# New call orders for the five engines of an attention and feed-forward kernel

## The reference

```python
q, k, v = x @ wq, x @ wk, x @ wv
q, k = rope(q) * D**-0.5, rope(k) * D**-0.5     # half of the features are rotated
p = softmax(causal_mask(q @ k.T))               # one head of 128
x1 = layernorm(x + (p @ v) @ wo)
w1b = mean(abs(w1), axis=1) * sign(w1)          # binarized weights, w2 alike
h = gelu(x1 @ w1b.T + b1)
out = layernorm(x1 + h @ w2b.T + b2)
```

## Time and profile before

| | |
|---|---|
| median of 3 runs | 276.72 us (276.22 to 276.80) |
| profiled execution: span | 274.5 us |
| PE busy | 260.9 us, 95% of the span |
| PE weight loads | 208.7 us, 76% (beside the matmuls) |
| DVE busy | 229.6 us, 84% |
| ACT busy | 224.7 us, 82% |
| POOL busy | 167.2 us, 61% |
| DMA | 31.94 MB, mean 116 GB/s |
| chain that ended last | PE 81%, DVE 6%, ACT 5%, issue 3%, DMA 2% |

### The profile page before, as it was taken

The page is one execution under the profiler, slowest core; times in us unless marked ns, Lnnn a source line. Parts: engine busy times, 40 slices in busy tenths (PEclk is TensorE's granted clock), DMA queues, the critical chain, the costliest instruction groups (busy, mean ns, idle before and its releaser), DMA issues.

```text
span 274.5 us, 5184 instructions
## 1 busy us (share of the span) xinstructions
PE 260.9 (95%) x1485; PEld 208.7 (76%) x1487; DVE 229.6 (84%) x638; ACT 224.7 (82%) x398; POOL 167.2 (61%) x258
## 2 busy tenths in 40 slices
PE   7899999999999999999999999999999999999960
PEld 3678989987779588868879688868886878897630
DVE  2799999999999996999979987998689738537984
ACT  3378964565897989996998999898999799999972
POOL 3033132613625698399821998497819887887772
PEclk9999999999999999999999999999999999999997
DMA  7944596479657936833685318825830720200323
GB/s 178 166 61 87 107 145 98 115 163 192 104 132 160 199 94 153 180 47 78 173 187 127 82 39 249 184 71 151 189 73 27 197 55 2 76 2 0 111 90 108
DMA packets 58012, 31.94 MB, mean 116 GB/s; under 512 B 33408, under 2 KB 54400, under 8 KB 57984
## 3 DMA queue, kind: packets, MB, share of 16 engines
q1 hardware_dynamic: 57024, 30.76, 50.4%
q10 hardware_dynamic: 960, 0.85, 1.3%
HBM read 9.18 MB, written 4.19 MB: 49 GB/s over the span
## 4 chain that ended last, share of the span: by engine, by line
PE 81%; DVE 6%; ACT 5%; issue 3%; DMA 2%; ACTq 1%; POOL 0%; POOLq 0%
PE pair L589 18%; PE bank L606 18%; PE bank L632 5%; PE bank L674 4%; PE pair L650 4%; PE pair L651 4%; PE bank L620 4%; PE bank L682 4%; PE bank L683 4%; PE bank L719 2%; DMA sin_sb<-in_sin_dram 2%; PE pair L663 2%; PE pair L665 2%; PE pair L664 2%; PE bank L639 2%
## 5 line engine op out<-in xcount | busy, mean ns | idle before, releaser
L391 POOL TENSOR_TENSOR hid_lo<-hid,hid_hi 128x1024 fp32r<-128x1024 f32 x28 | 66.0, 2386 | 19.7 <-ACT hid_hi L1075 19.7
L1004 ACT ACTIVATE prob<-pair,negmax 128x128 f32<-128x128 f32 (+3 forms) x64 | 47.2, 742 | 14.2 <-DVE negmax L1457 12.5
L606 PE MATMUL bank<-probT,xa 128*128 128x512 f32 (+3 forms) x160 | 54.2, 482 | 0.0
L1457 DVE CUSTOM_DVE_ANT_0 pair<-pair,mask_row 128x128 f32<-128x128 f32 (+3 forms) x64 | 47.9, 759 | 6.1 <-PE pair L589 5.5
L606 PEld LDWEIGHTS bank<-probT,xa 128*128 128x128 f32 x160 | 29.1, 190 | 20.2 <-issue 15.3
L341 POOL TENSOR_TENSOR xT_lo<-xT,xT_hi 128x512 fp32r<-128x512 f32 x14 | 18.0, 1288 | 40.4 <-ACT xT_hi L1034 40.4
L1467 DVE STREAM_TRANSPOSE turned<-prob 128x128 f32<-128x128 f32 (+7 forms) x56 | 39.5, 724 | 0.5 <-ACT prob L1004 0.5
L589 PE MATMUL pair<-qkT_hi 128*128 128x512 f32 (+3 forms) x96 | 36.0, 375 | 0.8 <-DVE qkT_lo L1619 0.3
L1068 ACT ACTIVATE hid<-pair,b_sb,alpha 128x1024 f32<-128x1024 f32 x28 | 32.9, 1209 | 0.1
L589 PE MATMUL pair<-qkT_lo,qkT_hi 128*128 128x512 f32 (+3 forms) x96 | 32.8, 342 | 0.0
L589 PE MATMUL pair<-qkT_hi,qkT_lo 128*128 128x512 f32 (+3 forms) x96 | 32.8, 342 | 0.0
(11 more groups left out here) (116 smaller groups left out, 649.9 us busy)
## 6 DMA issues: line engine op xcount, KB each, us to landing
probT<-turned SPq DMA_DIRECT2D x96, 116.0 KB, 2.3
probT<-turned SPq DMA_DIRECT2D x128, 52.0 KB, 2.0
xq<-in_L_attn_x_dram SPq DMA_DIRECT2D x28, 128.0 KB, 4.0
xa<-in_L_attn_x_dram SPq DMA_DIRECT2D x7, 512.0 KB, 4.7
out_dram<-res SPq DMA_DIRECT2D x7, 512.0 KB, 3.3
hid<-in_L_ffn_w_dram SPq DMA_DIRECT2D x2, 256.0 KB, 3.2
out_dram<-res SPq DMA_DIRECT2D x2, 256.0 KB, 2.3
xa<-in_L_attn_x_dram SPq DMA_DIRECT2D x1, 256.0 KB, 3.6
```

Of the source, the lines that this page charges most:

```text
L391: pool.tensor_tensor(hid_lo[:, j, :], hid[:, j, :], hid_hi[:, j, :].bitcast(F32), ALU.subtract).then_inc(s_hid_lo[j], 1)
L606: ins = pe.matmul(bank_of["px", g, c][:, 0:n * P], xa[c % 2][:, j, :], probT[g][:, :, TG * j:TG * j + n, :].rearrange("p n m i -> p m n i" ...
L1004: act.activation(prob[r % 3][:, 0:(r + 1) * P], pair_of["score", r, c][:, slice(*columns(r))], ACT.Exp, scale=-1.0, bias=negmax[:, r:r + 1 ...
L1457: dve.tensor_tensor_reduce(mine, mine, mask_row[:, T - (r + 1) * P:T], -1.0, -MASKED, ALU.add, ALU.min, negmax[:, r:r + 1]).then_inc(s_max ...
```

## The change

Every engine's list has the same calls as before, in another order. The only other edit is a condition in `fill`, which is now also called before three pairs have been handed out. The full diff is some 900 lines long; below are all of SP, the opening of POOL, and those parts of the other lists of which the text speaks.

```diff
@@ -255,10 +255,10 @@
                 sp.dma_start(out[c].rearrange("(n p) d -> p n d", p=P)[:, ts, :], res2[c % 2][:, ts, :]
                              ).then_inc(s_stored[c % 2], 16)
 
+            tokens(1)
             stripes(2)
             carry(0, 0)
             stripes(3)
-            tokens(1)
             stripes(B - 4)
             carry(0, 1)
             carry(1, 1)
@@ -269,22 +269,22 @@
             stripes(B - 2)
             tokens(3)
             carry(0, 3)
+            stripes(B - 1)
             carry(1, 3)
-            stripes(B - 1)
+            tokens(B - 4)
             carry(0, B - 4)
-            tokens(B - 4)
-            tokens(B - 3)
+            store(0)
             carry(1, B - 4)
             carry(0, B - 3)
+            tokens(B - 3)
             tokens(B - 2)
-            store(0)
             carry(1, B - 3)
+            store(1)
             carry(0, B - 2)
-            store(1)
+            tokens(B - 1)
             carry(1, B - 2)
+            carry(0, B - 1)
             store(2)
-            tokens(B - 1)
-            carry(0, B - 1)
             store(3)
             store(B - 4)
             store(B - 3)
@@ -400,48 +400,48 @@
             rotation_sum(0, 2)
             xT_low(0, 3)
             xT_low(1, 3)
+            rotation_sum(1, 2)
             first_factors(0, 0)
-            rotation_sum(1, 2)
+            first_factors(1, 0)
             rotation_sum(0, 3)
-            first_factors(1, 0)
             xT_low(0, B - 4)
-            xT_low(1, B - 4)
             rotation_sum(1, 3)
             first_factors(0, 1)
+            xT_low(1, B - 4)
             first_factors(1, 1)
             rotation_sum(0, B - 4)
-            rotation_sum(1, B - 4)
             hidden_low(0, 0)
             hidden_low(1, 0)
+            xT_low(0, B - 3)
+            xT_low(1, B - 3)
             hidden_low(2, 0)
-            xT_low(0, B - 3)
             hidden_low(3, 0)
+            rotation_sum(1, B - 4)
+            hidden_low(0, 1)
             first_factors(0, 2)
-            xT_low(1, B - 3)
             first_factors(1, 2)
+            second_factors(0)
             rotation_sum(0, B - 3)
+            rotation_sum(1, B - 3)
...
@@ -556,7 +556,8 @@
 
             def fill(n):
 
-                wait_freed(*list(pair_of)[-len(pairs)])
+                if len(pair_of) >= len(pairs):
+                    wait_freed(*list(pair_of)[-len(pairs)])
                 for _ in range(n):
                     pe.matmul(pairs[len(pair_of) % len(pairs)][:, 0:BANK], warm[:, 0:P], warm[:, :], start=True, stop=True)
 
@@ -730,15 +731,15 @@
             turn_qk(1, 0)
             keep_warm(6)
             setup_turn_wv()
+            fill(2)
             scores(0, 0)
             scores(1, 0)
-            fill(2)
+            scores(2, 0)
+            setup_wvo()
             turn_qk(2, 0)
-            scores(2, 0)
             scores(3, 0)
-            setup_wvo()
+            turn_qk(3, 0)
             project(0, 1)
-            turn_qk(3, 0)
             project(1, 1)
...
             up(3, 0)
             scores(0, 3)
+            weigh_group(0, 0, 3, 2)
+            turn_x1(0, 1)
             scores(1, 3)
-            turn_qk(3, 3)
-            weigh_group(0, 0, 3, 2)
             scores(2, 3)
-            turn_x1(0, 1)
             scores(3, 3)
+            project_out(0, 2)
             scores(4, 3)
-            project_out(0, 2)
             project(1, B - 4)
             scores(5, 3)
+            turn_x1(1, 1)
+            weigh_group(1, 0, 3, 2)
+            weigh_group(1, 4, 7, 2)
             scores(6, 3)
-            weigh_group(1, 0, 3, 2)
-            turn_x1(1, 1)
-            weigh_group(1, 4, 7, 2)
             scores(7, 3)
             turn_qk(0, B - 4)
             turn_qk(1, B - 4)
             up(0, 1)
             up(1, 1)
             project_out(1, 2)
+            down(0, 0)
+            down(1, 0)
...
             weigh_row(6, B - 1)
+            turn_x1(0, B - 1)
             weigh_row(7, B - 1)
-            turn_x1(0, B - 1)
+            up_half(0, 0, B - 1)
             project_out(1, B - 1)
-            up_half(0, 0, B - 1)
             up_half(0, 1, B - 1)
             down(0, B - 2)
             down(1, B - 2)
             turn_x1(1, B - 1)
-            fill(7)
             turn_y(0, B - 2)
             turn_y(1, B - 2)
-            fill(2)
             up_half(1, 0, B - 1)
             up_half(1, 1, B - 1)
             down_quarter(0, 0, B - 1)
@@ -982,6 +981,8 @@
             down_quarter(2, 1, B - 1)
             down_quarter(3, 1, B - 1)
             turn_y(1, B - 1)
+            fill(7)
+            fill(2)
 
         @block.scalar
...
             xT_high(0, 1)
-            setup_signs()
+            xT_high(1, 1)
             exponentials(0, 0)
             exponentials(1, 0)
-            xT_high(1, 1)
             exponentials(2, 0)
-            exponentials(3, 0)
             qkT_high(2, 0)
             qkT_high(3, 0)
+            exponentials(3, 0)
+            setup_signs()
             setup_magnitudes()
...
             tok_copy(1, B - 3)
-            pxT_copy(0, 3)
+            second_norm(0, 0)
+            second_norm(1, 0)
+            second_norm(2, 0)
+            second_norm(3, 0)
+            x1T_high(0, 2)
             xT_high(0, B - 2)
-            xT_high(1, B - 2)
-            hidden_high(1, 1)
-            hidden_high(2, 1)
             exponentials(2, B - 4)
             exponentials(3, B - 4)
             exponentials(4, B - 4)
+            xT_high(1, B - 2)
+            x1T_high(1, 2)
+            hidden_high(2, 1)
             hidden_high(3, 1)
+            pxT_copy(1, 3)
             exponentials(5, B - 4)
-            pxT_copy(1, 3)
-            x1T_high(0, 2)
-            x1T_high(1, 2)
+            second_norm(4, 0)
+            second_norm(5, 0)
+            second_norm(6, 0)
             exponentials(6, B - 4)
+            second_norm(7, 0)
...
             gelu(2, 3)
-            gelu(3, 3)
-            tok_copy(0, B - 1)
-            y_half(1, 2)
-            exponentials(0, B - 2)
-            exponentials(1, B - 2)
-            hidden_high(0, 3)
-            pxT_copy(0, B - 3)
-            xT_high(1, B - 1)
-            exponentials(2, B - 2)
-            exponentials(3, B - 2)
-            exponentials(4, B - 2)
             second_norm(0, 1)
-            x1T_high(0, B - 4)
             second_norm(1, 1)
-            hidden_high(1, 3)
-            hidden_high(2, 3)
-            hidden_high(3, 3)
-            x1T_high(1, B - 4)
             second_norm(2, 1)
             second_norm(3, 1)
             second_norm(4, 1)
+            gelu(3, 3)
+            y_half(0, 2)
+            tok_copy(0, B - 1)
+            second_norm(5, 1)
+            y_half(1, 2)
+            second_norm(6, 1)
...
             second_norm(1, 2)
             second_norm(2, 2)
+            second_norm(3, 2)
+            second_norm(4, 2)
+            second_norm(5, 2)
             tok_copy(1, B - 1)
+            y_half(0, 3)
             y_half(1, 3)
-            second_norm(3, 2)
             gelu(2, B - 4)
+            second_norm(6, 2)
+            second_norm(7, 2)
...
@@ -1630,34 +1631,33 @@
             x_squares(0, 1)
             qkT_low(0, 0)
             qkT_low(1, 0)
-            first_rotation_sum(1)
+            x_squares(1, 1)
             setup_wvT()
             row_max(0, 0)
+            first_rotation_sum(1)
             row_max(1, 0)
-            x_squares(1, 1)
+            row_max(2, 0)
+            setup_wvo()
...
             rotate(0, 2)
-            row_max(2, 1)
             turn_row(0, 1)
             turn_row(1, 1)
+            row_max(2, 1)
+            row_max(3, 1)
             x_squares(0, 3)
             x_squares(1, 3)
-            row_max(3, 1)
             turn_row(2, 1)
             row_max(4, 1)
+            reciprocals(1, 0)
             turn_row(3, 1)
             row_max(5, 1)
-            turn_row(4, 1)
+            row_max(6, 1)
             residual1(0, 0)
             residual1(1, 0)
             residual1(2, 0)
             residual1(3, 0)
+            row_max(7, 1)
+            qkT_low(0, 2)
             statistics1(0, 0)
-            turn_row(5, 1)
-            row_max(6, 1)
-            row_max(7, 1)
-            reciprocals(0, 1)
+            statistics1(1, 0)
             rotate(1, 2)
-            statistics1(1, 0)
-            turn_row(6, 1)
+            x_squares(0, B - 4)
             statistics1(2, 0)
             statistics1(3, 0)
-            qkT_low(0, 2)
+            reciprocals(0, 1)
+            turn_row(4, 1)
+            qkT_low(1, 2)
+            turn_row(5, 1)
+            turn_row(6, 1)
             turn_row(7, 1)
-            x_squares(0, B - 4)
-            x_squares(1, B - 4)
-            qkT_low(1, 2)
...
```

More of the change, by code:

```diff
@@ L453, in _ @@
             hidden_low(0, B - 4)
+            second_factors(3)
             hidden_low(1, B - 4)
@@ L892, in _ @@
             scores(2, B - 2)
```

(71 more changed lines are left out.)

562 lines of the change are left out of this document (279 added, 283 removed).

## The result

The changed kernel takes 298.54 us (296.19 to 300.03), the kernel before 276.47 us beside it: a ratio of 1.078, interval 1.072 to 1.085, 22 us slower. The forecast was 278.0 with a range up to 281.0: the sign was right, the size was not, and the range missed the time by 17.5 us.

The account below looks back on a forecast made before the run. TensorE was taken to bound the middle, 30 to 230 us, leaving only head and tail to recover. 276.7 + 1.4 (batch 2) + 1.0 (ACT and POOL) − 1.1 (tail) + 0 (head) = 278.0 us, range 274.5 to 281.0.

Parts of the forecast that it names:

- the price of the lock: VectorE and GpSimd share a port pair, locked for a whole instruction; first_norms under a hidden_low would wait; not in the sum.
- one such wait, 2.4 us: Rival, much slower: a norm block, or a first_norm held by a hidden_low, uncovered on PE's path; about 280.5 us, chance 0.15.
- +2.5 for the middle: Upper bound of the term for ACT and POOL in the middle: one block of second_norms not covered at all.
- The wait at batch 2: PE's wait for carry(1,2) ahead of weigh_group(1,0..3,2), near 91 us, grows: +1.4 us, bounds +0.8 and +2.0.
- δ: Lateness of SP's chain of carries from DVE's new order: 0.6 to 1.2 us, 0 if DVE gains in the head.
- ACT's blocks of norms: Middle: second_norms in blocks of four to six delay ACT's work for PE, about 0.25 us each: +1.0, bounds 0 and +2.5.
- The tail: From 230 us: norms leave ACT's chain, PE work fills a wait, fills move to the end: −1.1 us, bounds 0 and −2.5.
- SP, nothing: SP's other edits, tokens(1) in the head, stripes(7) and stores ahead of carries, fall in idle queue time: no cost.
- The head, 0: first_rotation_sum(1) moves to about 15.5 us and misses or meets xT_low: booked 0, between −1.1 and +0.7 us.
- The clock: Rival: without the fills PE pauses in the tail and matmuls run at half clock, +3, about 281 us; chance 0.03.
- The forecast's own span: Range of the forecast alone, its bounds taken one at a time: 277.3 to 279.5 us; chance 0.37.

Follow-up runs that it names:

- norm_accum: Changed kernel with first_norm in a form that also writes out an accumulator, the factor 1/sqrt(var) left out: 277.59 us, ratio 1.002.
- its control: Kernel before with the accumulator form of first_norm, the factor 1/sqrt(var) left out: 276.26 us, ratio 0.998.
- norm_accum_old_sp: Changed kernel with the accumulator form of first_norm and SP's list of the kernel before: 277.00 us, ratio 1.000.
- hold_all: Changed kernel with seven waits more on POOL, ahead of each instruction that held a first_norm by 0.9 us or more: 280.67 us, ratio 1.013.
- before_head: Kernel before with only three DVE calls of the head in the new order, first_rotation_sum(1) behind them: 276.66 us, ratio 0.999.

## Why the prediction was wrong

**The step that failed is the price of the lock.** The prediction saw it in the head, named first_norm under hidden_low as the place where it would come back, put it at nothing in the sum, since no row of before showed it for the new order, and as a rival priced one such wait, 2.4 us, at a chance of 0.15. It was 14 waits of 20.6 us in all, five of them under xT_low and rotation_sum, which the prediction had not named for first_norm. PE waited 12.4 us for x in six waits, and 3.4 us of half clock followed two of those.

One wait was a guess where rows would have given a number. In before, POOL's three long operations take 66.0 us, 18.0 and 18.0 us of 274.5, at 2.39, 1.29 and 1.29 us each; a DVE instruction that starts at any time meets one with that share, and waits for half of it on average: (66.0 x 1.19 + 18.0 x 0.64 + 18.0 x 0.64) / 274.5 = 0.37 us. Times 64 first_norms that is 24 us, an estimate of DVE's lost time in an order that takes no heed of the lock; measured 20.6.

That the two come so close is partly luck: by the same shares 22 of the 64 would start under one of the three in the changed kernel; 16 did, and 14 were held, for longer than half. In before 2 start so, and none is held by more than 0.1 us (median 342 ns, longest 436): the old order avoids it everywhere. The right reading was: a reshuffle loses that unless each place is shown to keep it. The upper bound of the sum, +2.5 for the middle, left it out.

**What it did to the end.** DVE's wait alone would be hidden in part; its idle time was some 45 us (274.5 − 229.6). It came through because turn_x1 needs four first_norms in a row, and because hidden_highs were called earlier on ACT: POOL had hidden_lows in stock and ran them back to back (9.28 us for four at 253.66 us), so that three of the first four first_norms of batch 7 met one.

**The rest of the sum.** Without the lock the new order is at 277.59 us against 276.26 us, +1.3 us, where the sum said +1.3. That match is luck in part: their intervals overlap by a hair, and the terms are less good than their total.
- The wait at batch 2, +1.4: right in kind, at its lower bound. In norm_accum PE waits there, as this row shows, and PE's gap by the starts of its matmuls is 0.8 us against 0.2 in before; with SP's old list it is 1.3. δ was zero: carry(0,1) starts at 40.72 us, as DVE had gained 1 us in the head, which I had named as the condition. In the changed kernel itself this wait doesn't show, since PE comes later, held by 2.54 us for exponentials behind a held first_norm.

```profile
90.26 1.98 PE L608 MATMUL bank<-probT,xa 128*128 128x512 f32 x4 [0.66 <-DMA probT<-turned]
```

- ACT's blocks of norms, +1.0: too much. From 30 to 230 us PE is busy 198.59 of 200.00 us in norm_accum and 199.48 in its control. 0.6 of these 0.9 us are the wait above; at most 0.3 are left for the norms.
- The tail, −1.1: not seen in norm_accum. The last turn_y starts at 267.27 us there and at 266.28 us in the control, and the middle has lost 0.9 of that. Where the fills stood, PE waits for yT and x1T_lo, 0.51 and 0.69 us, as the prediction feared, and the clock is low behind them. In norm_accum_old_sp, where it is not, PE is busy 197.93 of the 200.00 us, 1.55 less than in the control, and its last turn_y starts at 267.13 us, 0.85 later: there the tail seems to give back 0.7 us. These are single executions, so its size is not shown.
- SP, nothing: stripes(7) ahead of carry(1,3) can cost 2.5 us of PE's time when batch 3 is tight (hold_all), 0.2 us when it isn't.
- The head, 0: right for the time (before_head). But first_rotation_sum(1) takes 0.78 us in the changed kernel, where the prediction looked for over 1.5; what DVE gained there went into δ.
- The clock, a rival of 3 us at 0.03: 3.4 us, but behind the held first_norms and not where the fills had stood. There it is mixed: in norm_accum the granted clock was 0.74 on average from 255 to 260 us, in norm_accum_old_sp 1.00 with nearly the same pauses, and putting the fills back brought no time.

The forecast's own span, 277.3 to 279.5, is not what its bounds one at a time give: with the tail at −2.5 that is 276.6.

What stays open: whether +1.3 us is exact, and how it divides between ACT's blocks and the tail; of the pieces taken singly, two gave worse orders and the head gave nothing.

## What to carry to other kernels

Where a long list of POOL instructions runs beside short DVE instructions that they can hold, look at the spread of each DVE line, not at its waits: a held instruction shows as a long one, and PE's wait behind it names DVE, not POOL. Before an order is changed, find which POOL instructions hold which DVE calls (here hidden_low, xT_low and rotation_sum, but not the powers), and multiply the number of these calls by the share of time of those POOL instructions and half their length. That is a rough price in DVE time of an order that doesn't look, tried here on one kernel; how much of it reaches the end depends on what waits for the calls. Where the computation allows a form of the DVE instruction that isn't held, it takes the question away; here, with a factor of the norm left out, it gave back 21 of 22 us, where seven waits put by hand gave 18.

## What the runs showed of the hardware

- Back-to-back POOL instructions let one DVE instruction through at each border: at 234.10 us the first three of eight first_norms needed 5.7 of their 6.99 us, as one followed each hidden_low.
- A POOL instruction that only writes holds a first_norm as well (0.90 us instead of 0.34, under a memset of 0.96 us).
- A POOL power on 128x4, 1.05 us in the profile, does not hold the first_norms that run within it (0.33 and 0.34 us); spans on POOL are rough, so how long it is at work on SBUF is not known.
- The accumulator form costs no more than the plain one at 128 columns: 338 ns against 340, and DVE is busy 230.0 us in both orders with it.
